# Pairing equal windows of two sequences in a windowed-attention and expert kernel

## What is computed

```
q, k, v = split_heads(x @ Wq + bq), split_heads(x @ Wk + bk), split_heads(x @ Wv + bv)   # 16 heads of 8
starts = jnp.arange(n_win) * 32 ;  idx = starts[:, None] + jnp.arange(64)
scores = einsum('bhnqd,bhnkd->bhnqk', q[:, :, idx], k[:, :, idx]) * scale + pos_bias[None, :, None]
ow     = einsum('bhnqk,bhnkd->bhnqd', softmax(scores), v[:, :, idx])
# the windows' outputs are added at their tokens and divided by how many windows hold the token
# (the last window is added twice and counted twice)
x = layernorm(x + merged @ Wo + bo)
topk_vals, topk_idx = top_k(x @ router_w.T, 2)          # gates: sigmoids, divided by their sum
x = layernorm(x + sum over e of gate_e * ((silu(x @ w_gate[e]) * (x @ w_up[e])) @ w_down[e]))
```

## Time and profile before

| | before |
|---|---|
| median of 3 runs | 747.44 us (747.14 to 749.71) |
| the profiled execution: its time | 748.15 us |
| its span in the trace | 746.4 us |
| PE busy | 642.8 us (86%) |
| PEld busy | 498.1 us (67%) |
| DVE busy | 509.5 us (68%) |
| ACT busy | 371.4 us (50%) |
| POOL busy | 461.6 us (62%) |

### The profile page before, as it was taken

The page is one execution under the profiler, slowest core; times in us unless marked ns, Lnnn a source line. Parts: engine busy times, 40 slices in busy tenths (PEclk is TensorE's granted clock), DMA queues, the critical chain, the costliest instruction groups (busy, mean ns, idle before and its releaser), DMA issues. The chain is left out here.

```text
span 746.4 us, 33384 instructions
## 1 busy us (share of the span) xinstructions
PE 642.8 (86%) x13242; PEld 498.1 (67%) x13242; DVE 509.5 (68%) x1553; ACT 371.4 (50%) x546; POOL 461.6 (62%) x624
## 2 busy tenths in 40 slices
PE   3689999999999999999999999899996999999000
PEld 1256666666667667667666667589995999998000
DVE  6834786776787686787786777757884566666086
ACT  2132444544444544544544434466774677775057
POOL 7620325645546546646646554668888888888655
PEclk8888999999999999999999999999998899999555
DMA  6893346446345445355455450224334333332296
GB/s 158 240 283 107 106 113 187 135 114 187 115 134 157 137 144 148 126 163 148 134 155 148 121 153 26 58 83 132 101 94 137 102 100 101 101 101 80 72 378 267
DMA packets 83577, 103.54 MB, mean 139 GB/s; under 512 B 15488, under 2 KB 70144, under 8 KB 83424
## 3 DMA queue, kind: packets, MB, share of 16 engines
q1 hardware_dynamic: 73344, 82.26, 37.9%
q0 software_dynamic: 8640, 17.84, 7.3%
q10 hardware_dynamic: 1440, 1.31, 0.5%
HBM read 60.12 MB, written 40.79 MB: 135 GB/s over the span
## 5 line engine op out<-in xcount | busy, mean ns | idle before, releaser
L296 POOL DMA_INDIRECT slots<-rows_sb,slot_at x128 | 127.9, 999 | 128.3 <-PE o_ps L1289 81.7
L816 DVE TENSOR_REDUCE neg_max<-score_ps 128x16 f32<-128x1024 f32 x109 | 133.2, 1222 | 85.6 <-PE score_ps L1233 83.9
L710 ACT ACTIVATE prob<-scoret_ps 128x1024 f32<-128x1024 f32 x109 | 111.6, 1024 | 137.1 <-PE scoret_ps L1233 137.1
L564 POOL DMA_INDIRECT results<-scaled_sb,result_at x142 | 139.3, 981 | 25.5 <-issue 14.1
L743 ACT CAST w_slot<-wgu_sb 128x1024 fp32r x71 | 74.6, 1051 | 0.2
L1289 PE MATMUL o_ps<-v_sb,prob 128*64 128x18 f32 x2048 | 70.8, 210 | 3.7 <-issue 3.7
L1289 PEld LDWEIGHTS o_ps<-v_sb,prob 128*64 128x64 f32 x2048 | 67.3, 139 | 4.3 <-issue 4.2
L1243 PE MATMUL score_ps<-bias_hl,fold 128*128 128x512 f16 x218 | 66.6, 388 | 3.1 <-DVE neg_max L816 3.1
L1249 PE MATMUL scoret_ps<-bias_hl,fold 128*128 128x512 f16 x218 | 66.1, 385 | 0.2 <-ACT prob L710 0.2
L689 ACT COPY v_sb<-bank 64x512 f32<-64x512 f32 (+1 forms) x64 | 36.0, 563 | 51.6 <-PE bank L1221 30.8
L1303 PE MATMUL ctx_ps<-diag,o_sb 128*64 128x64 f32 x896 | 51.8, 234 | 9.6 <-DVE o_sb L831 5.0
(11 more groups left out here) (186 smaller groups left out, 1587.1 us busy)
## 6 DMA issues: line engine op xcount, KB each, us to landing
stack<-scratch SPq DMA_DIRECT2D x32, 512.0 KB
blocks<-scratch SPq DMA_DIRECT2D x126, 128.0 KB
scratch<-qk_hl SPq DMA_DIRECT2D x120, 128.0 KB
xin<-slots SPq DMA_DIRECT2D x71, 130.0 KB
blocks<-results SPq DMA_DIRECT2D x16, 512.0 KB, 6.5
x_sb<-in_x SPq DMA_DIRECT2D x16, 256.0 KB
out<-y_sb SPq DMA_DIRECT2D x16, 256.0 KB, 3.8
results<-scaled_sb,result_at POOLq DMA_INDIRECT x142
```

Source lines behind the costliest of these rows:

```text
L296: nc.gpsimd.indirect_dma_start(slots, bass.IndirectOffsetOnAxis(ap=slot_at[:, k % 2, n:n + 1], axis=0), rows_sb[:, k % 2, n // TT, n % TT, ...
L564: pool.indirect_dma_start(results, bass.IndirectOffsetOnAxis(ap=result_at[s % RBUF][:, t:t + 1], axis=0), scaled_sb[:, s % RBUF, t, :], No ...
L710: act.activation(prob[:, (par + u) % 2, :], turned_scores(i, u)[:, :, :].rearrange("p b c -> p (b c)"), ACT.Exp).then_inc(exp_done, 1)
L816: dve.tensor_reduce(neg_max[:, par, :, v, :], ps[:, :, :].rearrange("p b (h k) -> p b h k", k=W), AX_X, ALU.max, negate=True).then_inc(max ...
```

## The change

A unit now holds the same window of both sequences of the step: `UNITS` is (w, w + 256) for w = 0, 32, ... 192.

- As both windows of a unit have the same shares, `context` is one matmul: all 128 columns of `o_sb` (window a, feature) against `diag` of both parities e (2 x 64 columns). It writes a two-part range of `ctx_ps`, whose partitions now say window and feature and whose columns say parity and token.
- `ctx_copy` is therefore four instructions of 64x256, from each (a, e) quarter to its place; `ctxt_ready` counts two to a step, and `project_out` waits for the second behind its second product. b_v has two columns and comes in two loads.
- x is turned in two orders: `xt_sb` holds it by (window start, sequence, token) for the windows at multiples of 64, the new tile `xt_odd` for those at odd multiples of 32, so each unit of `project_v` is one matmul. `xt_copy` has two instructions (128x512 and 128x384).
- q and k come out of `project_qk` in that order too, and `qk_copy` puts them back in that of the tokens.

```diff
-UNITS = [(0, 64), (128, 192), (256, 320), (384, 448), (32, 96), (288, 352), (160, 416)]
+UNITS = [(w, w + S) for w in range(0, S - W + 1, STRIDE)]
...
-        b_q, b_k, b_v, b_qs = (sb(n, [P, 1]) for n in ("b_q", "b_k", "b_v", "b_qs"))
+        b_q, b_k, b_qs = (sb(n, [P, 1]) for n in ("b_q", "b_k", "b_qs"))
+        b_v = sb("b_v", [P, 2])
...
+        xt_odd = sb("xt_odd", [P, 2, NU // 2 * P])
...
-        N_QK, N_CONST = 2, 4
+        N_QK, N_CONST = 2, 5
...
-                sp.dma_start(b_v[:, :], bv.rearrange("(p a) -> p a", a=1)).then_inc(consts_in, 16)
+                for a in range(2):
+                    sp.dma_start(b_v[64 * a:64 * a + 64, :], bv.rearrange("(e p) -> p e", e=2),
+                                 allow_slow_non_contiguous=True).then_inc(consts_in, 16)
...
-                    act.copy(xt_sb[:, par, :], bank[1][:, :]).then_inc(xt_ready, 1)
+                    sequences = bank[1][:, :].rearrange("p (a t) -> p a t", a=2)
+                    act.copy(xt_sb[:, par, :].rearrange("p (w a t) -> p a w t", a=2, t=W),
+                             sequences.rearrange("p a (w t) -> p a w t", t=W))
+                    act.copy(xt_odd[:, par, :].rearrange("p (w a t) -> p a w t", a=2, t=W),
+                             sequences[:, :, STRIDE:S - STRIDE].rearrange("p a (w t) -> p a w t", t=W)).then_inc(xt_ready, 1)
...
-                        act.activation(qk_f[:, n, :], bank[n][:, :], ACT.Identity, bias=b[:, :], scale=s).then_inc(qk_copied, 1)
+                        act.activation(qk_f[:, n, :].rearrange("p (a w t) -> p w a t", a=2, t=W),
+                                       bank[n][:, :].rearrange("p (w a t) -> p w a t", a=2, t=W),
+                                       ACT.Identity, bias=b[:, :], scale=s).then_inc(qk_copied, 1)
...
-                    act.activation(ctxt_sb[:, :], ctx_ps[:, :], ACT.Identity, bias=b_v[:, :], scale=1.0).then_inc(ctxt_ready, 1)
+                    for a in range(2):
+                        rows = slice(64 * a, 64 * a + 64)
+                        for e in range(2):
+                            last = act.activation(ctxt_sb[64 * e:64 * e + 64, a * S:(a + 1) * S], ctx_ps[rows, e * S:(e + 1) * S],
+                                                  ACT.Identity, bias=b_v[rows, e:e + 1], scale=1.0)
+                        last.then_inc(ctxt_ready, 1)
...
-                        a, b = UNITS[u]
-                        cols = slice((u - u0) * P, (u - u0 + 1) * P)
-                        if b == a + W:
-                            last = pe.matmul(bank[n][:, cols], xt_sb[:, par, a:a + P], w_v[:, :], start=True, stop=True)
-                        else:
-                            for r, t0 in ((0, a), (W, b)):
-                                last = pe.matmul(bank[n][r:r + W, cols], xt_sb[:, par, t0:t0 + W], w_v[:, :],
-                                                 start=True, stop=True)
+                        windows = (xt_sb, xt_odd)[u % 2][:, par, u // 2 * P:u // 2 * P + P]
+                        last = pe.matmul(bank[n][:, (u - u0) * P:(u - u0 + 1) * P], windows, w_v[:, :], start=True, stop=True)
...
-                        after(pe, ctxt_ready, i)
+                        after(pe, ctxt_ready, 2 * i)
                     settle(pe)
-                    for a in range(2):
-                        t0 = UNITS[u][a]
-                        for e in range(2):
-                            rows = slice(64 * e, 64 * e + 64)
-                            last = pe.matmul(ctx_ps[rows, t0:t0 + W],
-                                             o_sb[:, (par + u) % 2, a, :, :].rearrange("p h d -> p (h d)"),
-                                             diag[:, e, share(t0), :], start=(u == 0 and a == 0), stop=(u == NU - 1),
-                                             skip_group_check=True)
+                    w = UNITS[u][0]
+                    last = pe.matmul(ctx_ps[:, :].rearrange("p (e t) -> p e t", e=2)[:, :, w:w + W],
+                                     o_sb[:, (par + u) % 2, :, :, :].rearrange("p a h d -> p (a h d)"),
+                                     diag[:, :, share(w), :], start=(u == 0), stop=(u == NU - 1), skip_group_check=True)
                     last.then_inc(ctx_done, 1)
...
-                    pe.wait_ge(ctxt_ready, k + 1)
+                    pe.wait_ge(ctxt_ready, 2 * k + 1)
...
                     for t in range(TT):
+                        if t == TT // 2:
+                            pe.wait_ge(ctxt_ready, 2 * k + 2)
```

## The result

The kernel now takes 754.12 us (median of 8 runs, 750.64 to 757.83) against 747.89 (8 runs, 746.51 to 751.48) of the kernel before on the same chip: ratio 1.0073, 95% interval 1.0045 to 1.0100. So it is 0.73% slower, over the 0.5% that this kernel's measurement can tell, though the lower end of the interval lies just under it. The profiled execution took 755.23 us, with a span of 753.5.

The account below looks back on a forecast made before the run. PE's order was taken to bound steady attention. Per step, -0.16 us on PE and +0.15 at the boundary gave -0.01, or -0.2 over 15 boundaries; +0.6 at the start made +0.4, so 747.8 us, range 743.5 to 753.5.

Parts of the forecast that it names:

- rivals 1 and 2: Context copies don't overlap, spacing 0.49: 751.5 us, chance 0.12; each full-shape exit on PE costs 0.10: 752.7, chance 0.12.
- the case of both together: Context copies without overlap and full-shape exits on PE at 0.10 each: 756.4 us, chance 0.04.
- rival 4: V projection and unit savings vanish into PE's waits: +1.5 us, 749.3; chance 0.61 together with the forecast.
- The 0.046: Context on PE: cost in us of leaving the wide product for another tile shape, added to 0.25.
- rival 2: Context on PE: leaving the full shape costs 0.10 us at each exit, total 752.7 us; chance 0.12 alone.
- the middle of 0.38 and 0.49: Context copies on ACT: start-to-start spacing taken as 0.43 us, between overlapping and non-overlapping bounds.
- +0.39 for the boundary: Step boundary: PE's delay in us per step if the four context copies are spaced 0.49 apart.
- the spacing of 0.40: Context copies on ACT: page's estimate, 493 ns each, said to end the copies 0.12 us earlier than the middle.
- The V projection: PE: the seventh unit's two half-width products go, saving 0.07 us a step.
- The start's +0.6: Kernel start: the second b_v load delays later loads on SP's queue, +0.6 us once, bounds 0 and 1.2.
- Rival 3: PE gives back its busy time: 18 us less, 729.5; chance 0.11, nearly all for the milder version at 740.7.
- its mild form: Full-shape exits free on PE and copy spacing 0.38: -0.49 us a step, 740.7 us; nearly all of chance 0.11.

Follow-up runs that it names:

- e2_two_copies: Changed kernel with two 128x256 context copies instead of four 64x256, quarters left in the wrong order; ratio 1.0022 to the kernel before.
- e1_context_back: Changed kernel with the earlier four context products, one 128x512 copy and one b_v load restored; ratio 0.9981 to the kernel before.
- e4_context_moved: Changed kernel with the context product of units 0 to 3 and 5 moved ahead of the 64*64 score products; ratio 1.0216 to the kernel before.
- c1_after_again: The changed kernel, unedited, run again on another chip; ratio 1.0017 to the kernel before.
- e9_copies_interleaved: Changed kernel with ACT's first exp between two pairs of copies, x turned first, last two output-projection products later; ratio 1.0382 to the kernel before.
- after: The changed kernel itself, as profiled with the result; median 754.12 us, ratio 1.0073 to the kernel before.

## Why the forecast came out as it did

**What came.** "No change" at 747.8 us was the forecast, and slower by 0.7% came. By the ratio that is 752.9 us against the 747.44 that the prediction started from. It lies within the stated range, which ended at 753.5, but only because that range was drawn to take in rivals 1 and 2. Both came true in part, the case of both together being priced at 756.4 and 4 in 100. The forecast itself (0.61 with rival 4) did not come: it had the step 0.01 us shorter, and the step is 0.40 longer.

**What failed.** Two terms of the sum were too small. On PE it is the wide product: "before value products a new unit should take 0.25 + 0.046 = 0.297". It took 0.411 on average. The larger part of the miss is in the 0.25. A quarter of a group of four holds a quarter of one load of weights that nothing covers; a product by itself behind the scores pays all of it, 0.10 us. Two passes of 0.112 and that load are 0.32, and the exit adds 0.09 and not 0.046. The 0.046 was read off L1218 before L1221, and that row held the 0.09 already. Its load starts 0.21 ahead, under `bias_s`, so its two products are passes alone, 0.445 and not 0.50, and from the last of them to L1221 it is 0.205, as behind the new product. So rival 2 was nearly right about the exit, and what no rival priced is the load. The prediction named it in its last sentence ("a lone wide product that costs more than a quarter of four, for its weights can't load before norm is done"), with another reason. `norm` is not the reason behind the scores: the load begins with the product there in the same way as that of the output projection does, which has no `norm` to wait for.

**Context, term by term.** Four exits before 128*64 values: +0.08 forecast, 4 x (0.411 - 0.277) = +0.54 measured. Two before 128*32 values: -0.17 forecast, 2 x (0.418 - 0.381) = +0.07 measured. Before the bias product: -0.13 forecast, -0.08 measured. In sum +0.53 for a forecast of -0.22, in a step.

**Copies.** The second term is their spacing. Their duration was right: 474 ns forecast, 468 measured. The spacing was taken as the middle of 0.38 and 0.49; it is 0.484, the end that the half-height pair of L689 showed. The new copies are of half height too, and at full height (`e2_two_copies`) it is 0.37. With 0.49 the prediction's own working gives +0.39 for the boundary; measured are +0.42 in `project_out`, +0.065 in `turn_x` and -0.08 in the context's last unit, so +0.40. The working held, the choice in it did not. By the steps this is the term that costs the time: `e2_two_copies` is rid of it alone, and its step is back within 0.07 of the kernel before. One slip beside it: with the spacing of 0.40 and the 493 ns of its estimate from the page, the fourth copy would start 3 x 0.03 us earlier and last 0.02 longer, so it would end 0.07 earlier and not 0.12; the sum doesn't use it.

**What held.** The V projection: -0.07 forecast, -0.085 measured, -0.14 on the other chips. The second copy of x is hidden, the exp behind it waits for its scores as before. The permuted q and k cost nothing (`e1_context_back`). The start's +0.6 isn't to be seen beside a difference of 5.5 us that the clock made. Rival 3, PE giving back its busy time, is refuted: PE had 704 instructions fewer and was busy longer, and its mild form (free exits, spacing 0.38) is refuted by the 0.09 and the 0.484.

**What the sum missed.** By the measured terms the groups cost 0.785 us more in a step, 11.8 us in 15. Half of it came back, since the kernel before had some 0.4 us of waits in a step that the slower order fills. The prediction saw such giving back for a gain (its rival 4) and not for a loss.

**What is open.** Why the load of the wide product waits for the end of the scores and not for that of the bias product. The Trainium skill (TensorEngine Tiling, Key Properties) says that changing the tiling mode drains the engine. In `e4_context_moved` the product shares its shape with the group ahead, its load runs under that group, and it adds 0.22. In the change's place it is the only one of its shape, its load starts 0.09 behind the last one of the scores, and it adds 0.41: one change of shape more for 0.19. That agrees with the rule, as an entry whose load is laid bare and an exit; but no run changes the shape ahead and the one behind by themselves. Open, too, are how much of the dearer product would show in a kernel without PE's waits, and why the expert stage is longer on the other chips.

## What to carry to other kernels

Where one wide product takes the place of narrow ones that had the shape of their neighbours, price it as a lone product between two changes of shape (here 0.41 us: two passes, a load that nothing covers, an exit), not as a share of a group of four (0.25). Then ask which of the added costs falls where the engine waits anyway: here the dearer product did for the most part, and the copies, for which PE itself waits, did not. When two bounds of a cost are far apart, ask which row has the new instruction's shape, and take that end. And before work is moved to fill a gap, look at what else shifts with it: here every move won its 0.2 to 0.5 us locally and lost more, because outputs were read too early or because DVE came to run beside POOL.

## What the runs showed of the hardware

- Copies on ACT of 128 partitions overlap by 0.10 us (2 of 470 ns in 0.84, `e2_two_copies`); those of 64 partitions here don't (4 of 468 ns in 1.92). The Trainium skill (ScalarE: Activation LUTs, What ACT_TABLE_LOAD costs) tells of an overlap of about 93 ns for back-to-back instructions of 128 partitions; the full-height pair agrees, the half-height ones do not follow it.
- The same normalisation on DVE, f32 128x128 out of SBUF with two scalars from pointers, takes 343 ns (median) in `c1_after_again` where it touches no POOL instruction, and 817 in the mean in `e9_copies_interleaved`, where most of it runs beside POOL's split, up to 1.32 us for one. The Trainium skill (GPSIMD Engine Reference, 1. Specifications) says that GpSimd's interfaces to SBUF are shared with VectorE, with contention for some of its instructions. The rows fit that and give the price; which kind of instruction this one is, they don't show.
- A lone f32 128*128 product of 128 columns adds 0.22 us behind a group of its own shape and 0.41 between two groups of other shapes (`e4_context_moved`, `after`). Its first record is 273 ns where the load of its weights starts 0.21 ahead, and 377 where it starts with the product.
